# Softmax in a cross-attention and ternary feed-forward kernel: difference and scale in one VectorE step per tile, one exponential for four tiles, row sums on VectorE

## The chip, the cores and the metric

The kernel runs on 1 core of a Trainium2 chip. Its engines are TensorE (PE in the profile; PEld is its weight load), VectorE (DVE), ScalarE (ACT), GpSimd (POOL) and SyncE (SP), which issues the DMAs. The metric is the device time of one execution in microseconds; the time before is 446.84 us, the median of 3 runs (446.73 to 447.83). Less is better.

## The reference

For 8 batches of 512 rows of 512 numbers, a cross-attention over 64 context rows with a mask per batch, and then a feed-forward block with quantized activations and ternary weights:

```python
def xattn(h, mem, mask):            # h = layernorm(x), mem = ctx (8, 64, 512)
    scores = einsum('bsd,bmd->bsm', h, mem) / sqrt(512)
    scores = where(mask[:, None, :], scores, -1e30)
    attn = softmax(scores, axis=-1)
    return where(any(mask, -1)[:, None, None], einsum('bsm,bmd->bsd', attn, mem), 0)

def linear_bit(x, w, g):            # act_quant: to 8 bit by the row's largest; ternary_quant: to -1, 0, 1 times a scale
    return einsum('bsd,od->bso', act_quant(rmsnorm(x, g)), ternary_quant(w))

def ffn(h, w1, g1, w2, g2, w3, g3): # h = layernorm(x)
    return linear_bit(silu(linear_bit(h, w1, g1)) * linear_bit(h, w2, g2), w3, g3)

x = x + xattn(layernorm(x), ctx, mask)
x = x + ffn(layernorm(x), w1, g1, w2, g2, w3, g3)
```

## The kernel before

**Tiling.** Each batch is four tiles (TPB = 4) of 128 rows, 32 tiles in all. The feed-forward of a tile has four chunks (NCH = 4) of 512 hidden columns; the attention is done once for the four tiles of a batch, with tiles `sm`, `sd` and `prob` of 128 partitions x 4 tiles x 64 context rows.

**Order.** Nothing is scheduled by a planner: each engine has a program written out by hand, and semaphores tie them. Each engine runs `slot(b, j)` for tile j of batch b (`batches`, L300): slots of batch 0 from j = 2, a loop over batches 1 to 5, then batches 6 and 7 written out. In the slots of batch b the attention of batch b + 1 is made ahead, in pieces. All that lies ahead of the slots (weights brought in, scaled and clipped, attention of batches 0 and 1) is the start.

**The attention of batch a, in the order of time.** In tile 0 of batch a - 1: TensorE's `attention_ccT` and `attention_scores` (L1200), ScalarE's copy `half` (L663), TensorE's `attention_turn` (L1222); VectorE's `attention_softmax` (L881): add the mask (`sm`, L885), the largest of each row (`smax`, L888), the difference (`sd`, L892). The scores are made from x without the layernorm; the layernorm's 1/deviation comes in as the factor `rs`, one number per row and tile, which GpSimd makes in `attention` (L452 to L468) and ScalarE applies as the scale of the exponential. In tile 1: ScalarE's `attention_exp` (L665), four exponentials of 128x64, each with its own `scale` and with the row sum as an accumulated output (`psum_p`); TensorE's `attention_probT` (L1228), which transposes `prob`; ScalarE's copy `probT` (L676); VectorE's `attention_norm` (L896: reciprocal `rinv`, times `valid`: `rval`); the readout matmuls (L1243) and `attention_x1` (L904, L912), which adds the readout to X and gives the row sum of the result. The other half of the readout and of `x1` follows in tiles 2 and 3.

**The feed-forward around it.** `up` on TensorE (L1254) makes chunk n of a tile in two PSUM pairs S1 and S2; ScalarE's `silu` (L718, L724) reads S1, VectorE's gate product `gate` (L948, L954) multiplies with S2 and frees its bank (`s_hp_made`); GpSimd's `gain_3` (L526, L534) multiplies with g3 and VectorE's `max_3` (L957, L960) takes the largest. `stage_h_root`, `stage_h_factor` make the scale, ScalarE's `quantize_3` (L709, L716) quantizes the tile before, a DMA transposes it, `down` (L1281, L1297) multiplies it with W3, and VectorE's `result` (L989, L994) adds it to X. For the tile two ahead: GpSimd's `anm` (L477), which waits for that tile's x1 (`s_x1_made`), ScalarE's square (L706), GpSimd's root (L483, L488), VectorE's `ga` (`stage_a_gain`, L921, twice 128x512 with two SBUF operands), its largest (L927) and the factors (`stage_a_factor`, L939 to L945), and GpSimd's `quantize_12` (L517, L523).

**VectorE's slot** is: gate 0; `max_3` of chunk 3 of the tile before; `stage_h_top`, `stage_h_factor`; `stage_a_gain`; gate 1; (largest of `ga`, in tiles 0 to 2); gate 2; `worth_3`; `max_3` 0; `result`; gate 3; in tile 0 `attention_softmax`; `max_3` 1; `stage_a_factor`; in tile 1 `attention_norm`; in tile 2 `attention_cc`; in tile 3 the second half of x1; `max_3` 2; in tile 1 the first half of x1. **GpSimd's slot**: `gain_3` 3 of the tile before, `stage_h_root`, `anm`, `quantize_12`, `stage_a_worth`, `gain_3` 0, root, `gain_3` 1, in tile 0 `attention`, `gain_3` 2. **ScalarE's slot**: silu 0, square of the tile before, in tile 1 `attention_exp`, square for the tile two ahead, silu 1, in tile 1 the copy `probT`, in tile 0 `half` and two squares of x, then silu 2 and the two quantizations (in tiles 0 and 2 the quantizations first), silu 3, square.

The exponential and Silu lie in different activation tables, so ScalarE loads a table ahead of the exponentials and again ahead of the next Silu.

## Time and profile before

| | |
|---|---|
| median of 3 runs | 446.84 us |
| profiled execution | 446.26 us, span 444.5 us |
| mean granted TensorE clock | 0.953 |
| PE busy | 399.4 us, 90% |
| DVE busy | 404.4 us, 91% |
| ACT busy | 344.7 us, 78% |
| POOL busy | 338.4 us, 76% |
| DMA, mean rate | 149 GB/s |

The span runs from the first to the last instruction; about 2 us lie around it. A share of busy time is a mean over stages with different limits. A timeline row gives the start, the duration, the engine, the line, the operation, what it writes and reads, how many instructions are merged in the row, and in brackets the idle time before it with what ended it. Instructions of VectorE and ScalarE overlap at their ends: the next one often starts a little before the last one's duration is over.

### The profile page before, as it was taken

The page shows a single profiled execution, that of the slowest core. Times are in us where ns is not written, and L with a number is a line of the kernel's source. Part 1 is how long each engine was busy: PE and PEld are TensorE (multiplying, and loading weights), DVE is VectorE, ACT ScalarE, POOL GpSimd, SP SyncE. Part 2 cuts the span into 40 slices and gives each one's busy share as a digit, 9 for nine tenths or more (in the row PEclk, how much of TensorE's full clock was granted, in tenths as well). Part 3 has the DMA queues.
Part 4 walks back from the last instruction along what each step waited for, and adds up shares of the span by engine and source line. Part 5 has one row for each costly group of instructions (what it writes and reads, how often), then busy time and mean ns, then how long its engine had stood idle before and what let it go on. Part 6 is the DMA issues. An engine that isn't in the chain of part 4 may idle for free.

```text
span 444.5 us, 8267 instructions
## 1 busy us (share of the span) xinstructions
PE 399.4 (90%) x1870; PEld 178.8 (40%) x1870; DVE 404.4 (91%) x931; ACT 344.7 (78%) x618; POOL 338.4 (76%) x525
## 2 busy tenths in 40 slices
PE   8424695999999999999999999999999999999986
PEld 8101241334444443444344444444344434444433
DVE  5599799899999999999999999999999999999884
ACT  3678779786998689877988699868987796777651
POOL 0149888987878887878878787888788887888850
PEclk9755887999999999999999999999999999999999
DMA  6989861654774557734593477554774425354522
GB/s 263 400 300 368 296 188 24 154 94 112 188 174 100 119 117 188 179 80 106 161 204 80 111 184 179 97 118 107 191 183 76 114 57 113 83 113 98 113 66 79
DMA packets 110360, 66.41 MB, mean 149 GB/s; under 512 B 100736, under 2 KB 100864, under 8 KB 106752
## 3 DMA queue, kind: packets, MB, share of 16 engines
q1 hardware_dynamic: 110336, 66.14, 57.6%
q8 instruction: 8, 0.13, 0.1%
q14 instruction: 16, 0.13, 0.1%
HBM read 33.10 MB, written 8.39 MB: 93 GB/s over the span
## 4 chain that ended last, share of the span: by engine, by line
PE 55%; DVE 18%; issue 9%; ACT 8%; POOL 6%; DVEq 1%; DMA 1%; ACTq 0%; SPq 0%; POOLq 0%
PE S L1264 31%; PE DN L1297 16%; DVE hm L960 3%; PE R L1243 3%; DVE stageB L954 3%; ACT prob L671 2%; ACT L671 2%; POOL stageB L534 2%; PE DN L1305 2%; DVE wabs L1000 2%; DVE X L994 2%; ACT stageB L716 1%; POOL ser L563 1%; ACT junk_x L694 1%; DVE X L912 1%
## 5 line engine op out<-in xcount | busy, mean ns | idle before, releaser
L534 POOL TENSOR_TENSOR stageB<-stageB,g3b 128x512 f32<-128x512 f32 x127 | 163.1, 1292 | 32.2 <-DVE stageB L954 27.2
L1264 PE MATMUL S<-W2q,q12T 128*128 128x512 f16 x512 | 135.0, 387 | 6.0 <-DVE W2q L1029 3.6
L1264 PE MATMUL S<-W1q,q12T 128*128 128x512 f16 x512 | 134.9, 387 | 2.0 <-DVE W1q L1029 1.1
L1297 PE MATMUL DN<-W3q,stageB 128*128 128x512 f16 x496 | 122.1, 380 | 0.6 <-DVE X L994 0.3
L724 ACT ACTIVATE sg<-S,asc 128x512 f32<-128x512 f32 x128 | 87.0, 682 | 23.4 <-PE S L1264 19.7
L954 DVE TENSOR_TENSOR stageB<-sg,S 128x512 f32<-128x512 f32 x128 | 85.7, 675 | 5.9 <-ACT sg L724 4.3
L960 DVE TENSOR_REDUCE hm<-stageB 128x1 f32<-128x512 f32 x127 | 85.5, 674 | 0.1
L1264 PEld LDWEIGHTS S<-W2q,q12T 128*128 128x128 f16 x512 | 50.0, 99 | 71.5 <-DVE stageB L954 7.2
L1264 PEld LDWEIGHTS S<-W1q,q12T 128*128 128x128 f16 x512 | 48.9, 99 | 70.1 <-ACT sg L724 10.3
L731 ACT ACTIVATE junk<-stageB 128x1024 bf16<-128x1024 f32 x64 | 67.3, 1052 | 9.6 <-DVE stageB L954 9.5
L1297 PEld LDWEIGHTS DN<-W3q,stageB 128*128 128x128 f16 x496 | 48.0, 98 | 59.1 <-issue 1.6
L716 ACT ACTIVATE stageB<-stageB,hf 128x1024 f16<-128x1024 f32 x61 | 66.8, 1142 | 5.1 <-DVE hf L980 5.1
L921 DVE SCALAR_TENSOR_TENSOR ga<-X,anm,g12b 128x512 f32<-128x512 f32 x64 | 54.2, 886 | 2.4 <-POOL c L523 0.7
L523 POOL TENSOR_SCALAR c<-ga,af 128x512 f16<-128x512 f32 x64 | 45.2, 718 | 7.5 <-DVE af L945 7.4
L706 ACT ACTIVATE junk_a<-X,anm 128x512 bf16 (+1 forms) x32 | 23.0, 718 | 26.3 <-POOL anm L477 26.3
L927 DVE TENSOR_REDUCE am<-ga 128x2 f32<-128x1024 f32 x32 | 38.5, 1205 | 0.0
L488 POOL TENSOR_TENSOR ak<-avk,mhalf 128x1 f32<-128x1 f32 x32 | 27.3, 853 | 2.7
L994 DVE SCALAR_TENSOR_TENSOR X<-DN,hsc,X 128x512 f32 (+1 forms) x31 | 22.8, 737 | 2.9 <-PE DN L1297 2.9
L912 DVE SCALAR_TENSOR_TENSOR X<-R,rval,X 128x512 f32 (+1 forms) x32 | 22.6, 745 | 2.4 <-PE R L1243 2.4
L1243 PE MATMUL R<-ctxr,probT 64*128 64x512 f32 x64 | 20.9, 734 | 2.2 <-ACT probT L676 2.2
L544 POOL TENSOR_TENSOR hk<-hve,mhalf 128x1 f32<-128x1 f32 x32 | 17.6, 549 | 2.7
L483 POOL TENSOR_SCALAR avk<-avs 128x1 f32<-128x1 f32 x32 | 15.4, 481 | 3.8 <-ACT junk_a L706 1.0
(125 smaller groups left out, 425.5 us busy)
## 6 DMA issues: line engine op xcount, KB each, us to landing
X<-in_x SPq DMA_DIRECT2D x8, 1024.0 KB, 6.1
out_x<-X SPq DMA_DIRECT2D x32, 256.0 KB, 2.8
xTs<-in_xT SPq DMA_DIRECT2D x7, 1024.0 KB, 7.1
X<-in_w1T SPq DMA_DIRECT2D x4, 1024.0 KB, 10.5
stageB<-in_w2T SPq DMA_DIRECT2D x4, 1024.0 KB, 18.7
X<-in_w3T SPq DMA_DIRECT2D x4, 1024.0 KB, 9.1
ctxr<-in_ctx SPq DMA_DIRECT2D x16, 128.0 KB, 3.0
ctxc<-in_ctx SPq DMA_DIRECT2D x8, 128.0 KB, 4.4
```

Of the source, the lines that this page charges most:

```text
L523: nc.gpsimd.tensor_scalar(c12[:, i * D:(i + 1) * D], ga[:, i, :], af[:, i:i + 1], QUANTUM, ALU.mult, ALU.mult).then_inc(s_c12_made, 1)
L534: nc.gpsimd.tensor_tensor(gh[q][:, part], hp[:, part], g3b[:, part], ALU.mult).then_inc(s_gh_made, 1)
L716: nc.scalar.activation(c3[:, part], gh[q][:, part], ACT.Copy, scale=hf[:, :]).then_inc(s_c3_made, 1)
L724: nc.scalar.activation(sg[n % 2][:, :], S1[n % 2][:, :], ACT.Silu, scale=asc[z][:, 0:1])\
L731: nc.scalar.activation(junk[:, h * HALF:(h + 1) * HALF], hp[:, h * HALF:(h + 1) * HALF], ACT.Square, accum_out=hss[:, h:h + 1]).then_inc(s ...
L921: nc.vector.scalar_tensor_tensor(out=ga[:, i, :], in0=xtile(t), scalar=anm[:, :], in1=g12b[:, i, :], op0=ALU.add, op1=ALU.mult).then_inc(s ...
L927: nc.vector.tensor_reduce(am[:, :], ga[:, :, :], AX_X, ALU.max, apply_absolute_value=True)\
L954: nc.vector.tensor_tensor(hp[:, n * CH:(n + 1) * CH], sg[n % 2][:, :], S2[n % 2][:, :], ALU.mult)\
L960: nc.vector.tensor_reduce(hm[:, n:n + 1], gh[q][:, n * CH:(n + 1) * CH], AX_X, ALU.max, apply_absolute_value=True).then_inc(s_gh_max, 1)
L1243: mm = nc.tensor.matmul(R[e][:, :], probT[e * M:(e + 1) * M, i, :], ctxr[e * M:(e + 1) * M, :], start=True, stop=True)
L1264: mm = nc.tensor.matmul(bank[n % 2][:, :], q12T[q][:, i * KD + k, :], w[:, n, k, :], start=(k == 0), stop=(k == KD - 1))
L1297: mm = nc.tensor.matmul(bank[:, :], q3T[:, k, :], W3q[:, k, :], start=(k == 0), stop=(k == KH - 1))
```

## The change

Four edits that belong together:

- On VectorE `sd` is no longer one broadcast subtraction over 128x256. Four tensor_scalar instructions, one for each tile of 128x64, subtract the tile's `smax` and multiply by its `rs`. VectorE waits for `rs` (`s_rs_made`) there; ScalarE no longer does.
- On ScalarE the four exponentials of 128x64 with scale and accumulated row sum become one of 128x256 without either.
- On VectorE `attention_norm` first makes the row sums `psum_p` with a tensor_reduce over `prob`, and the reciprocal waits for it (`s_psum_made`).
- `s_prob_made` is raised once a batch, not four times, and all who wait for it (GpSimd, VectorE, TensorE) wait for the new count.

```diff
--- before.py
+++ after.py
@@ -232,6 +232,7 @@
         s_smax_made = sem("smax_made")
         s_sd_made = sem("sd_made")
         s_prob_made = sem("prob_made")
+        s_psum_made = sem("psum_made")
         s_rinv_made = sem("rinv_made")
         s_rval_made = sem("rval_made")
         s_probT_ps = sem("probT_ps")
@@ -461,7 +462,7 @@
                 nc.gpsimd.tensor_scalar(xve[:, :], var, scale, LN_EPS, ALU.mult, ALU.add).then_inc(s_x_ve, 1)
                 pool.wait_ge(s_x_ve, a + 1)
                 if later(a):
-                    pool.wait_ge(s_prob_made, TPB * a)
+                    pool.wait_ge(s_prob_made, a)
                 nc.gpsimd.tensor_tensor(xrs[:, :], xve[:, :], mhalf[:, :], ALU.pow).then_inc(s_x_rs, 1)
                 pool.wait_ge(s_x_rs, a + 1)
                 pool.nop(nofuse=True)
@@ -663,13 +664,10 @@
                 nc.scalar.copy(half[:, :], R[1][:, 0:TPB // 2 * P]).then_inc(s_half_made, 1)
 
             def attention_exp(a):
-                act.wait_ge(s_rs_made, a + 1)
                 act.wait_ge(s_sd_made, a + 1)
                 if later(a):
                     act.wait_ge(s_probT_ps, a)
-                for j in range(TPB):
-                    nc.scalar.activation(prob[:, j, :], sd[:, j, :], ACT.Exp, scale=rs[:, j:j + 1],
-                                         accum_out=psum_p[:, j:j + 1]).then_inc(s_prob_made, 1)
+                nc.scalar.activation(prob[:, :, :], sd[:, :, :], ACT.Exp).then_inc(s_prob_made, 1)
 
             def attention_probT(a):
                 act.wait_ge(s_probT_ps, a + 1)
@@ -888,14 +886,18 @@
                 nc.vector.tensor_reduce(smax[:, :], sm[:, :, :], AX_X, ALU.max).then_inc(s_smax_made, 1)
                 dve.wait_ge(s_smax_made, a + 1)
                 if later(a):
-                    dve.wait_ge(s_prob_made, TPB * a)
-                nc.vector.tensor_tensor(sd[:, :, :], sm[:, :, :],
-                                        smax[:, :].rearrange("p (j o) -> p j o", o=1).broadcast_to([P, TPB, M]),
-                                        ALU.subtract).then_inc(s_sd_made, 1)
+                    dve.wait_ge(s_prob_made, a)
+                dve.wait_ge(s_rs_made, a + 1)
+                for j in range(TPB):
+                    ins = nc.vector.tensor_scalar(sd[:, j, :], sm[:, j, :], smax[:, j:j + 1], rs[:, j:j + 1],
+                                                  ALU.subtract, ALU.mult)
+                ins.then_inc(s_sd_made, 1)
 
             def attention_norm(a):
 
-                dve.wait_ge(s_prob_made, TPB * (a + 1))
+                dve.wait_ge(s_prob_made, a + 1)
+                nc.vector.tensor_reduce(psum_p[:, :], prob[:, :, :], AX_X, ALU.add).then_inc(s_psum_made, 1)
+                dve.wait_ge(s_psum_made, a + 1)
                 nc.vector.reciprocal(rinv[:, :], psum_p[:, :]).then_inc(s_rinv_made, 1)
                 dve.wait_ge(s_rinv_made, a + 1)
                 nc.vector.tensor_scalar(rval[:, :], rinv[:, :], valid[:, bass.ds(a, 1)], None, ALU.mult)\
@@ -1226,7 +1228,7 @@
                 mm.then_inc(s_scores_ps, 1)
 
             def attention_probT(a):
-                pe.wait_ge(s_prob_made, TPB * (a + 1))
+                pe.wait_ge(s_prob_made, a + 1)
                 for i in range(TPB // 2):
                     mm = nc.tensor.transpose(R[0][:, i * P:(i + 1) * P],
                                              prob[:, 2 * i:2 * i + 2, :].rearrange("p j m -> p (j m)"), identf[:, :])
```

## Rows read from the trace of the kernel before

**Rows 1.** Busy time by stretch: length; PE, PEld, DVE, ACT, POOL; PEclk, DMA share, GB/s

```profile
128.00:176.00 48.00, 46.90 (x225) 20.71 (x224) 45.76 (x108) 40.26 (x77) 39.34 (x61) 1.00 0.60 139
```

**Rows 2.** Waits in one batch period: who, for whom: us in total, times, longest

```profile
PE R L1231 <- ACT prob L671: 1.1, 1, 1.1
...
DVE stageB L954 <- ACT sg L724: 0.6, 1, 0.6
```

**Rows 3.** The chain of waits around the exponentials: start, us, what

```profile
166.70 1.10 ACT prob L671 x6
```

**Rows 4.** Timeline of one core, from tile 3 to the next tile 0

```profile
194.88 1.27 DVE L954 TENSOR_TENSOR stageB<-sg,S 128x512 f32<-128x512 f32 x2
...
195.61 1.04 PE L1264 MATMUL S<-W2q,q12T 128*128 128x512 f16 x4
...
204.33 0.37 ACT L663 COPY half<-R 128x256 f32<-128x256 f32 x1 [0.55 <-PE R L1210]
...
208.90 0.69 DVE L954 TENSOR_TENSOR stageB<-sg,S 128x512 f32<-128x512 f32 x1 [0.61 <-ACT sg L724]
```

**Rows 5.** Timeline of tile 2; last, all instructions of L921: min/median/max ns

```profile
180.81 1.27 POOL L534 TENSOR_TENSOR stageB<-stageB,g3b 128x512 f32<-128x512 f32 x1
...
181.39 1.25 DVE L921 SCALAR_TENSOR_TENSOR ga<-X,anm,g12b 128x512 f32<-128x512 f32 x1
...
L921 DVE SCALAR_TENSOR_TENSOR ga<-X,anm,g12b x64: 737/751/1557, 21.3 to 407.1; 128x512 f32<-128x512 f32 x64
```

**Rows 6.** Timeline of the softmax of one batch, and the next batch's `sd`

```profile
162.21 2.50 POOL L534 TENSOR_TENSOR stageB<-stageB,g3b 128x512 f32<-128x512 f32 x2
...
163.71 0.42 DVE L888 TENSOR_REDUCE smax<-sm 128x4 f32<-128x256 f32 x1
...
164.26 0.73 DVE L892 TENSOR_TENSOR sd<-sm,smax 128x256 f32<-128x256 f32 x1
...
164.92 0.67 DVE L960 TENSOR_REDUCE hm<-stageB 128x1 f32<-128x512 f32 x1
...
166.35 0.35 ACT L671 ACTIVATE prob<-sd,rs 128x64 f32<-128x64 f32 x1
...
167.84 0.44 PE L1231 MATMUL R<-identf,prob 128*128 128x128 f32 x2 [1.08 <-ACT prob L671]
...
212.47 0.73 DVE L892 TENSOR_TENSOR sd<-sm,smax 128x256 f32<-128x256 f32 x1
```

**Rows 7.** Instructions of single lines: count, min/median/max ns, first and last start

```profile
L863 DVE TENSOR_SCALAR cc<-ctxc,cmean,mcol x8: 537/539/542, 6.6 to 334.7; 64x512 f32<-64x512 f32 x8
...
L1014 DVE TENSOR_SCALAR arg<-wsum x3: 133/133/134, 24.9 to 63.5; 128x1 f32<-128x1 f32 x3
...
L676 ACT COPY probT<-R x8: 350/364/373, 17.3 to 363.1; 128x256 f32<-128x256 f32 x8
...
L892 DVE TENSOR_TENSOR sd<-sm,smax x8: 424/734/837, 14.6 to 356.9; 128x256 f32<-128x256 f32 x8
...
L1022 DVE TENSOR_SCALAR W2q<-stageB,winv x1: 2341/2341/2341, 36.4 to 36.4; 128x2048 int16<-128x2048 f32 x1
L1022 DVE TENSOR_SCALAR W3q<-X,winv x1: 1278/1278/1278, 73.5 to 73.5; 128x2048 int16<-128x2048 f32 x1
```

**Rows 8.** Timeline of the row factors, the first x1 and GpSimd's next mean

```profile
176.66 0.17 DVE L899 RECIPROCAL rinv<-psum_p 128x4 f32<-128x4 f32 x1
...
178.37 0.08 DVE L912 DVE_READ_ACCUMULATOR X<-R,rval,X 128x1 f32 x1
...
178.72 0.19 POOL L477 TENSOR_SCALAR anm<-x1sum 128x1 f32<-128x1 f32 x1
```

**Rows 9.** Timeline: three waits, of the start, of batch 1 and of the tail

```profile
19.92 0.75 DVE L912 SCALAR_TENSOR_TENSOR X<-R,rval,X 128x512 f32<-128x512 f32 x1 [2.40 <-PE R L1243]
...
88.60 0.69 DVE L954 TENSOR_TENSOR stageB<-sg,S 128x512 f32<-128x512 f32 x1 [0.75 <-ACT sg L724]
...
401.64 1.04 PE L1297 MATMUL DN<-W3q,stageB 128*128 128x512 f16 x4 [0.34 <-DVE X L994]
```

## The prediction

> **What bounds the kernel now.** I read the busy shares by stretch first: in a middle stretch of 48 us TensorE is busy 46.9 us at a granted clock of 1.00 and VectorE 45.8 us [rows 1]. Neither has room to speak of, so shares cannot decide; the waits must. The waits of one batch period (48.21 us from one `sd` step to the next, from 164.26) name two: TensorE stands 1.1 us before the transposes of `prob` for the exponentials, and VectorE stands 0.6 us before one gate product for `sg` [rows 2]. The chain of waits passes through the exponentials [rows 3], which would make them worth 1 us a batch. The question is whether TensorE's time gained there reaches the end.
>
> It does not by itself. In tile 3 of each batch TensorE's second half of the last up projection starts at 195.61, and VectorE's gate product that frees its PSUM bank started at 194.88, as the first of a merged pair of 1.27 us, so it ended at about 195.55 [rows 4]. TensorE waits there for VectorE again, by some 0.1 us. From there the way is fixed: matmuls without a pause until the scores land, `half` on ScalarE at 204.33 (idle before it, waiting for the scores), two squares, the two quantizations and the third Silu, and the gate product at 208.90 after 0.61 us of waiting [rows 4]. From 194.88 to 208.90 are 14.0 us, in which nothing of the change lies. From 208.90 to the same gate product of the next batch (243.09, one period later) VectorE has no wait that the wait view shows. So the cycle that sets the period is VectorE, 34.2 us, and then this fixed 14.0 us. Whatever the change adds to VectorE between, which is both its edits, is paid; what it takes from ScalarE or TensorE there only makes TensorE wait longer at 195.61.
>
> One thing softens this: VectorE has waits that no view calls waits. When GpSimd runs its two-input product `gain_3`, a VectorE step with two SBUF operands lasts until GpSimd's is over: GpSimd's ended at 182.08, VectorE's `ga`, started 181.39, ended 182.64, 1.25 us long instead of 0.74 [rows 5]. `sd` is the same case: GpSimd's pair ended at 164.71, `sd` at 164.99, 0.28 us later, and it took 0.73 where the first batch has 0.42 [rows 6, 7]. One-input steps are held as well where they run at two columns a step: the scaling of 2048 columns took 2.34 beside GpSimd and 1.28 without [rows 7]. The Trainium skill, Advanced Engine Details and Errata, section VectorE Performance Modes, says that the second VectorE port is shared and that GpSimd and two-port instructions block each other; the trace agrees (0.28 and 0.56 us behind GpSimd's end).
>
> **The change part by part.**
>
> *One exponential.* From the first of four exponentials to TensorE's transpose: 167.84 - 166.35 = 1.49 us [rows 6]. One step of 256 columns: the copy of 256 columns takes 0.36 [rows 7], from SBUF I take 0.40 (an estimate), 0.44 with the hand-over. It saves 1.05 us of ScalarE a batch, between 0.9 and 1.1. The table load before it stays; if the compiler moves it ahead of the wait, another 1 us comes off, in the same hidden place.
>
> *`sd` as four tensor_scalar steps with two per-partition scalars.* The nearest row is `cc`, the same form over 512 columns: 0.54 [rows 7]. A step of one column without such a scalar takes 0.13 [rows 7], a reduction of 256 columns 0.42 [rows 6], some 1.1 ns a column; 512 columns at that rate would be 0.70, so `cc` runs at about two columns a step, 0.27 us, and has 0.27 fixed. A step of 64 columns is then 0.30, and since steps start 0.07 before the one ahead ends (164.92 against 164.99 [rows 6]), 0.23 from start to start; bounds 0.13 (the one-column row) and 0.30. The first is held by GpSimd to 164.71, as now, so the next instruction starts at about 164.68 + 3 x 0.23 = 165.37 instead of 164.92: +0.46 us, bounds +0.1 and +0.9 (all four held by GpSimd's small steps that follow). `sd` ends 0.46 later too. The wait for `rs` moves here from ScalarE; queued behind it are the maximum of `gh` and the factor steps of the activation scale, and GpSimd's quantization waits for these. `rs` is made early by GpSimd, ahead of the pair of [rows 6], which starts 2 us before `sd`: no cost; if it were late, all of VectorE would stand.
>
> By the Trainium skill, VectorE: DVE Perf Modes, section on the TRN2 errata, a step costs 58 cycles plus its columns over the mode's factor: 0.38 us for the four and 0.33 for the one, +0.05 instead of my +0.46, and the total would be 2.5 us less. Its rules for authors, on the other hand, ask for few instructions, which speaks against four for one. The measured 0.54 of `cc` does not fit 0.34 by that formula, so I keep the row.
>
> *Row sums.* A reduction of 128x256 like `smax`, 0.42, and the reciprocal now waits for it: 0.45 from start to start, at most the 0.55 between `smax` and `sd`, which has two waits [rows 6]. It stands ahead of `rinv` at 176.66 [rows 8]. The accumulator reads leave ScalarE (in the 1.05).
>
> *Sum on VectorE.* 0.46 + 0.45 = 0.91 us a batch. Behind it the `ga` of tile 2 at 181.39 had 0.51 us of hidden waiting for GpSimd [rows 5], which could absorb as much. But that GpSimd product comes at the end of a queue that starts with `anm` at 178.72, and `anm` needs the first `x1`, whose accumulator is read at 178.37 and 0.08 later is there [rows 8]: 178.45, now +0.91 = 179.36, so `anm` starts at about 179.45, 0.73 late, and the product with it. `ga` ends 0.73 late. So 0.73 a batch, and the other holds of `ga` follow GpSimd steps that VectorE itself releases and move along.
>
> *How often.* Batches 2 to 7: 6 x 0.73 = +4.4. Batch 1 pays 0.3 to 0.9 but has VectorE waiting 0.75 at 88.60 for a ScalarE and GpSimd queue that does not depend on it [rows 9]: 0. Batch 0 is on the way of the start: `sd` without a hold takes 0.62 more, the exponentials 1.05 less, and VectorE waits 2.40 us for the readout [rows 9], in which the reduction hides: -0.45, bounds -0.5 and 0. In the tail TensorE waits for VectorE's `X` at 401.64 [rows 9], so the delay is handed on in full.
>
> Total +4.4 - 0.45 = +3.9. The profiled execution was 446.26 us (span 444.5), the median of the runs 446.84: 450.2 or 450.7; I say 450.5.
>
> **The rivals.**
>
> *Held waits absorb it.* If GpSimd's queue in tile 2 goes by ScalarE's square instead of `anm`, VectorE gets 0.51 of its 0.91 back: 0.40 a batch, +1.95, 448.5. For it: the hold itself; against: the 178.45 against 178.72.
>
> *The 0.6 us wait goes.* If the Silu before 208.90 comes earlier because TensorE is ahead, the period grows by 0.91 - 0.69 = 0.2: +0.9, 447.4, no change. Against: the freeing gate at 195.55 fixes TensorE's lead.
>
> *TensorE is the bound (faster).* The chain of waits goes by the exponentials. If the 0.1 us at 195.61 were no true coupling and VectorE had room, each batch would win 1.05 - 0.46 = 0.59: 6 x 0.59 + 0.45 = 4.0, 442.6. It decides where the product at 194.88 ends later than TensorE is ready; only if it ends earlier is this right.
>
> *Dearer small steps.* If GpSimd's small steps hold each of the four, `sd` costs 0.9 and with the sum and fewer favours 1.1 a batch: +6.2, 452.8.
>
> That the edits don't do what they say I leave out: each replaced instruction has its row.
>
> **How the numbers follow.** Forecast 0.45, absorbed 0.14, wait gone 0.14, faster 0.13, dearer 0.14. Range 447.0 to 453.2, from the case of no change to the dear one; the faster case is left out. 0.3% (1.3 us) is about what a measurement here can tell: faster 0.13; same 0.17 (the third case and the low edge of the second); slower 0.70.
>
> **What would show it.** In the changed profile: one exponential of about 0.40; four steps of about 0.30 where `sd` was; a reduction of 0.42 before the reciprocal; TensorE's wait for `prob` gone or small and a longer one for VectorE's gate at the end of tile 3; a period of 48.9 instead of 48.21; the wait of 0.6 before the same gate product kept. The forecast is wrong if that last wait shrinks, if `ga` of tile 2 is no longer held, or if the period stays below 48.3.

## The result, and the profile after

The changed kernel takes 452.27 us, the median of 4 runs (452.02 to 452.93), against 446.79 (446.73 to 447.83, 4 runs) of the kernel before: ratio 1.0127, 95% interval 1.0114 to 1.0141, slower. The profiled execution took 452.02 us, its span 450.2 us against 444.5: +5.7 us, where the forecast's sum had +3.9. Two single executions among those of the experiments took 539.93 and 610.21 us, at granted clocks of 0.735 and 0.647; the ranges below leave them out.

Where the 5.7 us lie is read from one step that every batch has once, the maximum `smax`. Its rows of batches 1, 2 and 7 in the timeline, first of the kernel before, then of the changed one:

```profile
65.34 0.42 DVE L888 TENSOR_REDUCE smax<-sm 128x4 f32<-128x256 f32 x1
...
115.49 0.42 DVE L888 TENSOR_REDUCE smax<-sm 128x4 f32<-128x256 f32 x1
...
356.42 0.42 DVE L888 TENSOR_REDUCE smax<-sm 128x4 f32<-128x256 f32 x1
```

```profile
64.41 0.42 DVE L886 TENSOR_REDUCE smax<-sm 128x4 f32<-128x256 f32 x1
...
116.10 0.42 DVE L886 TENSOR_REDUCE smax<-sm 128x4 f32<-128x256 f32 x1
...
361.80 0.42 DVE L886 TENSOR_REDUCE smax<-sm 128x4 f32<-128x256 f32 x1
```

The difference is -0.93 at batch 1 (the start gained), +0.61 at batch 2 (batch 1 lost 1.54), +5.38 at batch 7: five periods that lost 4.77, 0.95 each (49.17 us instead of 48.22, the last one 49.01 for 48.05). The last 0.3 to 0.4 us come in batch 7 and the tail. So three terms: the period as the main one, batch 1, and the start.

**The softmax in the middle.** Timeline of the changed kernel; it answers [rows 6]:

```profile
163.78 2.50 POOL L535 TENSOR_TENSOR stageB<-stageB,g3b 128x512 f32<-128x512 f32 x2
...
165.26 0.42 DVE L886 TENSOR_REDUCE smax<-sm 128x4 f32<-128x256 f32 x1
...
165.72 1.27 DVE L892 TENSOR_SCALAR sd<-sm,smax,rs 128x64 f32<-128x64 f32 x4
...
166.91 0.67 DVE L962 TENSOR_REDUCE hm<-stageB 128x1 f32<-128x512 f32 x1
...
167.39 0.42 ACT L670 ACTIVATE prob<-sd 128x256 f32<-128x256 f32 x1
...
168.15 0.38 PE L1233 MATMUL R<-identf,prob 128*128 128x128 f32 x2
```

From `smax` to the next step `hm` VectorE takes 1.65 us, where it took 1.21 [rows 6]: +0.44 for the four steps. The one exponential takes 0.42 us, and TensorE's transposes no longer wait (no bracket behind the row; 1.08 before). The rest of the batch answers [rows 5, 8]:

```profile
178.67 0.41 DVE L899 TENSOR_REDUCE psum_p<-prob 128x4 f32<-128x256 f32 x1
...
179.11 0.18 DVE L901 RECIPROCAL rinv<-psum_p 128x4 f32<-128x4 f32 x1
...
180.84 0.08 DVE L914 DVE_READ_ACCUMULATOR X<-R,rval,X 128x1 f32 x1
...
181.19 0.19 POOL L478 TENSOR_SCALAR anm<-x1sum 128x1 f32<-128x1 f32 x1 [1.27 <-DVE X L914]
...
183.30 1.27 POOL L535 TENSOR_TENSOR stageB<-stageB,g3b 128x512 f32<-128x512 f32 x1
...
183.86 1.25 DVE L923 SCALAR_TENSOR_TENSOR ga<-X,anm,g12b 128x512 f32<-128x512 f32 x1
```

The row sums put 0.44 us ahead of the reciprocal. GpSimd's `anm` now waits 1.27 us for the first `x1`, and the product behind it still holds `ga` for 1.25 us: nothing of that hidden wait was given back.

**The waits and the fixed way.** Waits of the changed kernel over one period (175 to 224), then its timeline from tile 3 on; they answer [rows 2] and [rows 4]:

```profile
PE S L1266 <- DVE stageB L956: 1.1, 4, 0.4
DVE stageB L956 <- ACT sg L722: 0.6, 1, 0.6
PE R L1245 <- DVE X L914: 0.6, 1, 0.6
```

```profile
197.39 1.27 DVE L956 TENSOR_TENSOR stageB<-sg,S 128x512 f32<-128x512 f32 x2
...
198.12 1.04 PE L1266 MATMUL S<-W2q,q12T 128*128 128x512 f16 x4 [0.21 <-DVE stageB L956]
...
211.41 0.69 DVE L956 TENSOR_TENSOR stageB<-sg,S 128x512 f32<-128x512 f32 x1 [0.58 <-ACT sg L722]
```

TensorE's wait for the exponentials (1.1) has become 1.1 us of waits for VectorE's gate products and 0.6 for its `x1`. The way from the pair of gate products to the gate product at its end, after the scores, is 14.02 us, as before, and the wait at its end is 0.58 (0.61 before). In the profile's chain of waits VectorE has gone from 18 to 52% of the span and TensorE from 55 to 21%: the same cycle, but with TensorE now visibly behind VectorE.

**Batch 1.** The first fence is the timeline of the kernel before, the second the changed kernel's; the last line there groups the four steps of L892 between 61 and 68 us (min/median/max ns):

```profile
65.07 2.69 POOL L534 TENSOR_TENSOR stageB<-stageB,g3b 128x512 f32<-128x512 f32 x2
...
65.79 0.84 DVE L892 TENSOR_TENSOR sd<-sm,smax 128x256 f32<-128x256 f32 x1
...
66.56 0.67 DVE L960 TENSOR_REDUCE hm<-stageB 128x1 f32<-128x512 f32 x1
```

```profile
64.29 2.49 POOL L535 TENSOR_TENSOR stageB<-stageB,g3b 128x512 f32<-128x512 f32 x2
...
64.87 2.41 DVE L892 TENSOR_SCALAR sd<-sm,smax,rs 128x64 f32<-128x64 f32 x4
...
67.20 0.67 DVE L962 TENSOR_REDUCE hm<-stageB 128x1 f32<-128x512 f32 x1
...
L892 DVE TENSOR_SCALAR sd<-sm,smax,rs x4: 301/522/1300, 64.9 to 67.0; 128x64 f32<-128x64 f32 x4
```

The four steps took 2.41 us instead of 0.84. Of the four, two are 0.30 long, one 1.30, and so (the median being the mean of the middle two) one 0.74. The first product of GpSimd's pair ended at about 65.55: the 0.74 reaches from 64.87 to 65.61. The 1.30 reaches from about 65.54 to 66.84, and the second product ended at 66.78. So the narrow steps were held twice, by both products in turn.

Some 20 us later, still between `smax` 1 and `smax` 2, the same happens to two wide steps. The timeline of `ga`, in the kernel before and then in the changed one, where GpSimd's product comes between the two steps of the pair:

```profile
84.70 1.42 DVE L921 SCALAR_TENSOR_TENSOR ga<-X,anm,g12b 128x512 f32<-128x512 f32 x2 [0.65 <-POOL c L523]
```

```profile
85.13 2.43 DVE L923 SCALAR_TENSOR_TENSOR ga<-X,anm,g12b 128x512 f32<-128x512 f32 x2 [0.30 <-issue]
...
85.22 1.79 POOL L535 TENSOR_TENSOR stageB<-stageB,g3b 128x512 f32<-128x512 f32 x1
```

The pair takes 1.01 us longer, of which the shorter wait before it gives 0.35 back: 0.66 more, the second part of what batch 1 lost. Its third part is 0.16 for the row sums, of whose 0.44 the rest does not show there. VectorE's wait of 0.75 us at 88.60 [rows 9] is gone in the changed kernel and gives 0.83 back. The four steps themselves delay the next step by 1.57 (2.79 us from `smax` to `hm`, where it took 1.22). Together, 1.57 + 0.66 + 0.16 - 0.83 is 1.56, for the 1.54 us of above.

**The start.** Timeline of the kernel before, then of the changed one:

```profile
16.56 0.69 PE L1231 MATMUL R<-identf,prob 128*128 128x128 f32 x2 [2.96 <-ACT prob L671]
```

```profile
15.53 0.42 ACT L670 ACTIVATE prob<-sd 128x256 f32<-128x256 f32 x1 [0.56 <-DVE sd L892]
...
16.00 0.44 PE L1233 MATMUL R<-identf,prob 128*128 128x128 f32 x2 [2.44 <-ACT prob L670]
...
19.11 0.75 DVE L914 SCALAR_TENSOR_TENSOR X<-R,rval,X 128x512 f32<-128x512 f32 x1 [0.61 <-PE R L1245]
```

The transposes start 0.56 us earlier and are 0.25 shorter, and `x1` comes at 19.11 instead of 19.92 [rows 9]. The busy time of the stretch in which they fall (columns as in [rows 1]) shows why they are shorter; first the kernel before, then the changed one:

```profile
16.50:20.00 3.50, 2.77 (x6) 0.79 (x6) 1.07 (x4) 2.28 (x4) 0.00 (x0) 0.51 1.02 420
```

```profile
14.00:16.40 2.40, 0.40 (x2) 0.20 (x2) 2.33 (x7) 1.39 (x3) 0.00 (x0) 1.00 0.96 392
```

TensorE had been idle, and from about 16.5 us on its granted clock is 0.51, the level of 1.2 GHz, in both kernels. The transposes of the kernel before fell in the slow stretch, those of the changed kernel still ran at 2.4 GHz. That is luck and not the change: in the kept traces the clock falls anywhere from 14.6 to 17.6 us, and in the run of the changed kernel with `x1` moved (below), where it falls at 15.2, ahead of the transposes, the first `x1` comes 5.29 us after the first `smax`, not 5.06.

### The profile page after: what moved, and what is told of

It reads as the page before. It is cut to its first block, busy times and chain, and to the rows that moved or that the text cites. A ratio compares the mean times of both kernels' runs of the same rounds, so it can differ in the third digit from the quotient of the medians.

```text
span 450.2 us, 8238 instructions
## 1 busy us (share of the span) xinstructions
PE 400.4 (89%) x1870; PEld 176.7 (39%) x1870; DVE 413.5 (92%) x963; ACT 338.5 (75%) x562; POOL 337.6 (75%) x525
## 4 chain that ended last, share of the span: by engine, by line
DVE 52%; PE 21%; issue 16%; ACT 3%; DVEq 3%; POOL 2%; DMA 1%; SPq 0%; ACTq 0%; POOLq 0%
PE S L1266 11%; DVE hm L962 11%; DVE stageB L956 10%; PE DN L1299 5%; DVE ga L923 4%; DVE X L996 3%; DVE am L929 3%; DVE X L914 2%; DVE wabs L1002 2%; DVE sd L892 2%; PE DN L1307 2%; DVE aa L941 2%; DVE af L947 1%; ACT stageB L714 1%; DVE ha L976 1%
## 5 line engine op out<-in xcount | busy, mean ns | idle before, releaser
L1266 PEld LDWEIGHTS S<-W2q,q12T 128*128 128x128 f16 x512 | 48.0, 99 | 85.0 <-DVE stageB L956 25.9
L704 ACT ACTIVATE junk_a<-X,anm 128x512 bf16 (+1 forms) x32 | 23.1, 721 | 34.9 <-POOL anm L478 34.2
L478 POOL TENSOR_SCALAR anm<-x1sum 128x1 f32<-128x1 f32 x32 | 7.4, 231 | 16.7 <-DVE X L914 14.6
```

What stands on the lines that cost most here:

```text
L1266: mm = nc.tensor.matmul(bank[n % 2][:, :], q12T[q][:, i * KD + k, :], w[:, n, k, :], start=(k == 0), stop=(k == KD - 1))
```

## The experiments

Each ran beside the kernel before on the same chip (446.33 to 446.40 us there). The starts of the runs differ by up to 1.3 us from one another (the first `smax` comes at 13.22 to 14.55), so the verdict on a mechanism rests on the periods (from one `smax` to the next in the middle of the run), which agree within 0.05 us in a run, but for the first period of two kernels with a step moved (49.30 and 48.29), and the times stand beside them.

**The parts one at a time.** First the exponential alone:

```diff
+            nc.vector.memset(psum_p[:, :], 1.0)
...
-                for j in range(TPB):
-                    nc.scalar.activation(prob[:, j, :], sd[:, j, :], ACT.Exp, scale=rs[:, j:j + 1],
-                                         accum_out=psum_p[:, j:j + 1]).then_inc(s_prob_made, 1)
+                nc.scalar.activation(prob[:, :, :], sd[:, :, :], ACT.Exp).then_inc(s_prob_made, TPB)
```

> The kernel before, with one exponential of 128x256 in place of the four, and VectorE as it was. It leaves out the factor rs in the exponential and the row sums (a constant stands in for them), so that VectorE has not one instruction more. My theory (VectorE's order and the fixed way of 14.0 us behind the gate product of tile 3 set the period): the period stays at 48.2 us, TensorE's 1.1 us before the transposes of prob go and come back as waits for VectorE; only the start gains, some 1.2 us, so about 445.6 us. The rival (the chain of waits, TensorE as the bound): 1.05 us less in each of 6 batches as well, so 439 to 440 us and a period of about 47.2.

Measured: 444.39 us (444.27 to 448.8), ratio 0.9973 [0.9951, 0.9995], periods 48.22 to 48.23, unchanged. Its waits over one period:

```profile
DVE stageB L952 <- ACT sg L722: 0.6, 1, 0.6
PE S L1263 <- DVE stageB L952: 0.2, 1, 0.2
```

TensorE's 1.1 us before the transposes are down to 0.16, and nothing of it reached the period. Three waits for VectorE, 0.46 us in all (the longest is the 0.2 above), stand in its place; the rest shows as no wait. Of the 2.0 us that the profiled execution gains, 1.4 come from the start (`x1` at 18.47 instead of 19.92, 0.20 of it from the DMAs) and stand unchanged at `smax` of batch 7. The other 0.6 come behind it, where two holds of `ga` are shorter (1.28 and 1.19 us instead of 1.56 and 1.46); the theory had nothing there. That TensorE's 1.1 us are the bound is false.

Then `sd` alone: the changed kernel with four exponentials without scale, which keep the accumulated sums:

```diff
-                nc.scalar.activation(prob[:, :, :], sd[:, :, :], ACT.Exp).then_inc(s_prob_made, 1)
+                for j in range(TPB):
+                    ins = nc.scalar.activation(prob[:, j, :], sd[:, j, :], ACT.Exp, accum_out=psum_p[:, j:j + 1])
+                ins.then_inc(s_prob_made, 1)
...
-                nc.vector.tensor_reduce(psum_p[:, :], prob[:, :, :], AX_X, ALU.add).then_inc(s_psum_made, 1)
-                dve.wait_ge(s_psum_made, a + 1)
```

> The changed kernel, but with four exponentials of 128x64 that make the row sums as an accumulated output, and no reduction on VectorE: of the change only the four steps for difference and scale are left. Theory: 0.45 us more a period (48.7 us), 1 us or more in batch 1 where GpSimd's pair of products holds the first two of the four steps, and about 0.4 at the start: +3.8 us (2.8 to 4.5), so about 450.6. The rival (the price is mostly in the row sums, or in the hold of tile 2): +1.5 or less.

Measured: 449.35 us (449.0 to 450.41), ratio 1.0075 [1.0053, 1.0097], periods 48.71 to 48.73, +0.50; the +3.0 us lie in the expected range. In batch 1 its four steps took 2.23 us and pushed VectorE back by 1.39; the wait of 0.65 us before `ga` then gave 0.7 back and `ga` was not held, so `smax` 1 to `smax` 2 takes 0.65 us more than before, where the whole change costs 1.54.

And the row sums alone, on the kernel before:

```diff
-                    nc.scalar.activation(prob[:, j, :], sd[:, j, :], ACT.Exp, scale=rs[:, j:j + 1],
-                                         accum_out=psum_p[:, j:j + 1]).then_inc(s_prob_made, 1)
+                    nc.scalar.activation(prob[:, j, :], sd[:, j, :], ACT.Exp, scale=rs[:, j:j + 1]).then_inc(s_prob_made, 1)
...
+                nc.vector.tensor_reduce(psum_p[:, :], prob[:, :, :], AX_X, ALU.add).then_inc(s_psum_made, 1)
+                dve.wait_ge(s_psum_made, a + 1)
```

> The kernel before, with its four scaled exponentials, but without their accumulated sums; VectorE makes the row sums by a reduction as in the changed kernel. Theory: 0.44 us more a period (48.65 us), batch 1 nearly hidden, nothing at the start: +2.7 us (2.2 to 3.2), so about 449.5. With the start of the exponential alone, sd alone and sums alone should add up to the +5.5 of the whole change; if they do not, parts of it hide or double each other. The rival (the hold of ga in tile 2 takes the 0.44 in, as it has 0.5 us): below +0.8.

Measured: 448.01 us (447.82 to 449.23), ratio 1.005 [1.0033, 1.0067], periods 48.72 to 48.73, +0.50. Batch 1 costs it 0.17 us, nearly hidden as expected. Its +1.6 us lie below the expected range, 0.9 of that from first DMAs that landed earlier. In the period the parts add up to the whole: 0.50 + 0.50 + 0 against 0.95. In time they do not: -2.0, +3.0 and +1.6 make 2.6 of the 5.5 us. Earlier starts of the three make 1.3 of the difference. The other 1.6 are, in the traces, 0.6 before `smax` 1, 0.6 in batch 1 (only the whole change has `ga` held there) and 0.7 behind `smax` 7, less 0.3 in the periods; the first and the last of these were not followed.

**Batch 1.** To show what the narrow steps do, batch 1 alone gets back the one broadcast step. The changed kernel ran beside it once more: 451.79 us (451.04 to 452.5), ratio 1.0124 [1.0099, 1.015], periods 49.11 to 49.14.

```diff
                 dve.wait_ge(s_rs_made, a + 1)
+                if isinstance(a, int) and a == 1:
+                    nc.vector.tensor_tensor(sd[:, :, :], sm[:, :, :],
+                                            smax[:, :].rearrange("p (j o) -> p j o", o=1).broadcast_to([P, TPB, M]),
+                                            ALU.subtract).then_inc(s_sd_made, 1)
+                    return
```

> The changed kernel, but batch 1 alone makes its difference in one broadcast subtraction of 256 columns, without the factor rs (which batch 1 then lacks); batches 0 and 2 to 7 keep the four steps. Theory (the four narrow steps of batch 1 fall beside a pair of GpSimd's two-input products, and between them the second product gets in, so that two are waited for one after the other): the jump of 1.57 us at batch 1's difference falls to under 0.2, since a single step gets in between the two products as it does before; the sums and what follows keep theirs, so smax of batch 2 comes 0.5 to 1.5 us earlier than in the changed kernel (116.1), periods stay 49.17, and the time is 0.5 to 1.5 us below that of the changed kernel run beside it. Rival (batch 1's loss is the extra work and the moved half-speed stretch of the clock): the jump falls by the 0.46 of the middle batches at most, the time by at most 0.4.

Measured: 450.66 us (450.31 to 451.3), ratio to the kernel before 1.0098 [1.0077, 1.012]. Its timeline of batch 1:

```profile
64.12 2.68 POOL L535 TENSOR_TENSOR stageB<-stageB,g3b 128x512 f32<-128x512 f32 x2
...
64.70 0.97 DVE L892 TENSOR_TENSOR sd<-sm,smax 128x256 f32<-128x256 f32 x1
...
65.59 0.67 DVE L967 TENSOR_REDUCE hm<-stageB 128x1 f32<-128x512 f32 x1
```

From `sd` to `hm` 0.89 us instead of 2.33, and the jump against the kernel before is 0.14 instead of 1.57. GpSimd's pair is 0.19 us longer (2.68, as the 2.69 before, against 2.49): the single step is held by the first product and then gets in ahead of the second, for which GpSimd waits; the narrow ones end, and the second product gets in between them. 

Both traces have the same stretches at a granted clock of 0.5, about 16 to 47 and 67 to 74 us, in the run beside it 1.4 us later, and only one has the loss: the rival, the extra work and the moved stretch, is out. From the gate products ahead of `sd` to the one at 88.60, batch 1 now costs 0.17 us against the kernel before, where it costs 1.35 in the run beside it: with the hold at `sd`, that of `ga` is gone too, and the wait of 0.75 us is back. But of these 1.2 us only 0.42 are left from `smax` 1 to `smax` 2 (51.21 us against 51.63). 0.73 went in one place, two rows of the same run:

```profile
91.47 1.02 PE L1304 MATMUL DN<-W3q,stageB 128*128 128x512 f16 x4 [1.66 <-DMA stageB<-stageB]
...
112.42 0.69 DVE L961 TENSOR_TENSOR stageB<-sg,S 128x512 f32<-128x512 f32 x1 [1.34 <-ACT sg L722]
```

TensorE waited 1.66 us for the DMA that transposes the quantized tile; the transposes between 84 and 92 us took 4.8 us to land, in the run beside it 3.2, and there TensorE had no such wait. It was late from then on, and at the end of the fixed way VectorE waited 1.34 us instead of 0.61. So the hold is shown in place and size, 1.2 us; that the later transposes are what took 0.73 of it back is read from one trace. In the time the run gains 1.1 us, but its first `smax` is 0.7 us earlier, so the time does not show what the removal is worth.

The Trainium skill, SBUF — State Buffer, section Who interferes with whom, says that VectorE and GpSimd share a pair of ports by an exclusive lock. The traces agree for a lock per instruction: 0.74 and 1.30 us for two steps that take 0.30 alone.

**Can the hidden wait of `ga` be had back?** The forecast's rival said that it absorbs part of the cost. Two kernels put the first half of `x1` ahead of the maximum of chunk 2 in tile 1, so that GpSimd's `anm` comes earlier; once on the changed kernel, once on the kernel before:

```diff
-                max_3(t, 2, j % 2)
                 if attn and j == 1:
                     attention_x1(b + 1, 0)
+                max_3(t, 2, j % 2)
```

> The changed kernel, with one step moved on VectorE: in tile 1 the first half of x1 stands before the maximum of chunk 2, not behind it (0.6 us earlier); nothing is left out. Theory (GpSimd's anm waits for that x1, its product of tile 2 hangs behind anm, and that product holds VectorE's ga for 0.5 us): anm and the product 0.6 us earlier, the hold of ga in tile 2 gone, 0.5 us less in each of 6 periods than the changed kernel: 48.65 us a period, about 449.2 us in all. The rival (the hold costs nothing, or another GpSimd step holds instead): as the changed kernel, 452.2.

> The kernel before, with the same step moved on VectorE (in tile 1 the first half of x1 ahead of the maximum of chunk 2); nothing left out. In the changed kernel the move took the hold of 0.51 us away, but x1 then started 0.35 us after its turn, since it waits right behind rval. Theory: before, anm waits for GpSimd's own root as much as for x1 (the root is over at 178.59, anm starts at 178.72), so anm can come only some 0.05 us sooner, the hold stays near 0.45, and the 0.35 is paid: 48.5 us a period, +1.5 us in all, about 448. The rival (anm hangs on x1 alone): the hold goes and the period falls to 48.05, about 445.5.

Measured: on the changed kernel 450.65 us (450.39 to 450.88), ratio to the kernel before 1.0102 [1.0085, 1.0119], periods 48.97 to 49.00 (-0.17 to -0.2 against 49.17); on the kernel before 446.0 (445.48 to 446.78), ratio 0.999 [0.998, 1.0], periods 48.17 to 48.19 (-0.04). Timeline of the second:

```profile
177.46 0.75 DVE L912 SCALAR_TENSOR_TENSOR X<-R,rval,X 128x512 f32 x1 [0.25 <-DVE rval L901]
...
178.69 0.19 POOL L477 TENSOR_SCALAR anm<-x1sum 128x1 f32<-128x1 f32 x1
...
180.77 1.28 POOL L534 TENSOR_TENSOR stageB<-stageB,g3b 128x512 f32<-128x512 f32 x1
...
181.75 1.51 DVE L921 SCALAR_TENSOR_TENSOR ga<-X,anm,g12b 128x512 f32<-128x512 f32 x2
```

On the changed kernel `anm` and the product behind it come 0.3 us earlier in the period. But `x1`, directly behind `rval`, which it reads, now waits 0.24 us for it, and VectorE reaches `ga` 0.3 us later: the maximum had covered that hand-over. `ga` starts as the product ends and is not held; 0.5 of hold less 0.3 of delay is the measured gain of 0.2, where 0.5 was expected.

On the kernel before both the theory and its rival missed. The theory was right that `anm` does not hang on `x1` alone: `x1` comes 0.24 us earlier and `anm` only 0.03 (178.69 for 178.72 [rows 8]), right behind GpSimd's own root, which is over at 178.61. So the product stays where it was (180.77 for 180.81 [rows 5]). But the delay of VectorE was not paid: `ga` starts 0.36 us later than before, but the pair takes 1.51 us instead of 1.91 and is over at 183.26 for 183.30. The hold took the 0.36 in. That is the case in which the forecast's rival is right: a hold absorbs what VectorE adds behind the step that releases GpSimd (here `x1`), and nothing of what it adds ahead of it, since then GpSimd's product comes later too.

**Cheaper ways to the same end.** If VectorE's time sets the period, less work on it must shorten the kernel. First the difference made by ScalarE, as the bias of its four exponentials, with only -smax*rs (128x4) on VectorE:

```diff
-                nc.vector.tensor_tensor(sd[:, :, :], sm[:, :, :],
-                                        smax[:, :].rearrange("p (j o) -> p j o", o=1).broadcast_to([P, TPB, M]),
-                                        ALU.subtract).then_inc(s_sd_made, 1)
+                dve.wait_ge(s_rs_made, a + 1)
+                nc.vector.scalar_tensor_tensor(out=nb[:, :], in0=smax[:, :], scalar=-1.0, in1=rs[:, :],
+                                               op0=ALU.mult, op1=ALU.mult).then_inc(s_sd_made, 1)
...
+                    nc.scalar.activation(prob[:, j, :], sm[:, j, :], ACT.Exp, scale=rs[:, j:j + 1],
+                                         bias=nb[:, j:j + 1],
```

> The kernel before, with the difference taken off VectorE altogether: VectorE makes only minus smax times rs (128x4), and the four exponentials on ScalarE take it as their bias, with rs as the scale, straight from sm; sums accumulated as before. Masked scores are 65536 below, not 1e30. Theory: the 128x4 product has two SBUF operands and is held by GpSimd's pair until 164.71 like sd was, so VectorE wins only the 256 columns, 0.25 us a period: 47.95 us, and with the start about -1.5 us, 444.9. ScalarE gets 0.1 us more for each exponential and nothing depends on it. The rival (no hold for so small a step): 0.5 us a period, 443.5. If TensorE's wait for the exponentials counts: slower than before, since they take 0.4 us more.

Measured: 445.47 us (444.5 to 446.12), ratio 0.9974 [0.9963, 0.9986], periods 47.99 to 48.00, -0.22. Timeline:

```profile
161.63 2.51 POOL L534 TENSOR_TENSOR stageB<-stageB,g3b 128x512 f32<-128x512 f32 x2
...
163.59 0.57 DVE L893 SCALAR_TENSOR_TENSOR nb<-smax,rs 128x4 f32<-128x4 f32 x1
```

A step of 4 columns takes 0.57 us: it ends at 164.16, GpSimd's pair at 164.14. The hold doesn't care for the size of the step, so 256 columns less bring only 0.22.

Second the mask added by ScalarE, as a per-partition bias in its copy `half` (context rows are partitions there); VectorE's `sm` step goes, and `smax` and `sd` read the scores in PSUM:

```diff
-                nc.scalar.copy(half[:, :], R[1][:, 0:TPB // 2 * P]).then_inc(s_half_made, 1)
+                nc.scalar.activation(half[:, :], R[1][:, 0:TPB // 2 * P], ACT.Identity,
+                                     bias=mbT[:, bass.ds(a, 1)]).then_inc(s_half_made, 1)
...
-                nc.vector.tensor_tensor(sm[:, :, :], R[1][:, 0:TPB * M].rearrange("p (j m) -> p j m", j=TPB), bias,
-                                        ALU.add).then_inc(s_scores_made, 1)
-                dve.wait_ge(s_scores_made, a + 1)
-                nc.vector.tensor_reduce(smax[:, :], sm[:, :, :], AX_X, ALU.max).then_inc(s_smax_made, 1)
+                sm = R[1][:, 0:TPB * M].rearrange("p (j m) -> p j m", j=TPB)
+                nc.vector.tensor_reduce(smax[:, :], sm, AX_X, ALU.max).then_inc(s_smax_made, 1)
```

> The kernel before, with the mask added by ScalarE: the copy half becomes an Identity with a bias for each partition (there the context rows lie on the partitions), so VectorE's sm step goes, and smax and sd read the scores from PSUM. Theory: VectorE wins 0.45 us a period for sm and 0.3 for sd, which has one SBUF operand and so is not held any more: 0.75 us off VectorE in tile 0. But in tile 1 ga is held by a GpSimd product that can come only 0.26 us sooner (that long GpSimd waits for VectorE's af), so 0.3 to 0.5 us a period come through: 47.8 us, and about 443.5 us in all. The rival (holds do not matter, VectorE's busy time does): 0.75 us a period, 441.5.

> Both: the mask added in half by ScalarE, and no difference on VectorE (minus smax times rs as the bias of four exponentials that read the scores from PSUM). Masked scores are 65536 below. VectorE's softmax is one reduction and one 128x4 step. Theory: 1.0 to 1.2 us off VectorE in tile 0, but the same GpSimd product in tile 1 lets only 0.3 to 0.5 through: as the kernel with the mask in half, within 0.5 us, about 443.3. The rival (VectorE's busy time decides): 1.1 us a period, below 440.

> The changed kernel, with the mask added by ScalarE in its copy half (a bias for each of the 128 partitions) in place of VectorE's sm step; smax and the four sd steps read the scores in PSUM. Theory (VectorE's time between the gates sets the period, whatever it consists of): 0.27 off the period as the same edit gave on the kernel before, 48.9 instead of 49.17; and since smax and the four steps now start about 0.45 earlier, beside the end of GpSimd's pair, the first or first two of them are held, which could take back up to 0.5: period 48.9, range 48.8 to 49.3; time 1.5 us below the changed kernel, 0 to 2.5. Rival (reading scores in PSUM frees the four steps from the hold): period 48.5 or less, time 3 us or more below.

Measured: on the kernel before 444.67 us (444.07 to 445.45), ratio 0.9964 [0.9952, 0.9975], periods 47.95 to 47.96 (-0.27; 443.5 and 47.8 were expected), faster than both kernels. With the bias of the run above added, 446.29 (445.85 to 447.58), ratio 0.9998 [0.9986, 1.001], periods 48.12 to 48.13: worse, against what was expected. On the changed kernel 449.12 (448.81 to 449.42), ratio to the kernel before 1.0068 [1.0046, 1.009], 2.7 us below the changed kernel beside it, where 0 to 2.5 were expected, periods 48.87 to 48.88, -0.24 to -0.26. Timelines of the first, the second and the third:

```profile
162.91 2.66 POOL L533 TENSOR_TENSOR stageB<-stageB,g3b 128x512 f32<-128x512 f32 x2
...
164.68 0.42 DVE L891 TENSOR_TENSOR sd<-R,smax 128x256 f32<-128x256 f32 x1
...
169.37 2.08 DVE L920 SCALAR_TENSOR_TENSOR ga<-X,anm,g12b 128x512 f32<-128x512 f32 x2
```

```profile
164.97 0.82 DVE L893 SCALAR_TENSOR_TENSOR nb<-smax,rs 128x4 f32<-128x4 f32 x1 [0.21 <-DVE smax L888]
```

```profile
162.13 2.69 POOL L534 TENSOR_TENSOR stageB<-stageB,g3b 128x512 f32<-128x512 f32 x2
...
163.99 1.10 DVE L891 TENSOR_SCALAR sd<-R,smax,rs 128x64 f32<-128x64 f32 x4 [0.20 <-DVE smax L885]
```

With one operand in PSUM `sd` is not held: 0.42 us in the middle of GpSimd's pair, where it took 0.73 [rows 6], and the four narrow steps 1.10 instead of 1.27, beside a pair that runs to 164.82. In the second kernel the 4-column step, whose two operands lie in SBUF, is held again, for 0.82 us, and costs more than the 256 columns that it replaces. Of the 0.76 us that the edit takes from VectorE (0.45 for `sm`, 0.31 of hold) 0.27 reach the period: `ga` of tile 1 is held 0.30 longer (2.08 instead of 1.78), and VectorE's wait for `sg` grew from 0.6 to 0.8. For the third kernel the period of the theory came, but its reason, that the first steps would be held, did not. In batch 1 its steps were free too: from `smax` 1 to `smax` 2 it takes 50.32 us, in the changed kernel beside it 51.63. So moving the operand to PSUM takes 1.3 us off batch 1 (the missing `sm` step included), as the one wide step took 1.2 off up to the transposes: two different edits that both remove the hold remove the loss. The five periods bring another 1.3.

## Why the prediction was right, and where its sizes were off

**The mechanism held.** The bound was named as VectorE's 34.2 us and a fixed way of 14.0 us. The way stayed 14.02 us, its last wait 0.58, and the exponential's saving alone left the period as it was (48.22 to 48.23). Of what was to be seen, the exponential (0.42 for 0.40), the four steps (0.30 each), the reduction (0.41) and the wait kept came as said, and TensorE waits for VectorE's gates as forecast; that it now also waits 0.56 us for `x1` was not foreseen. The period is 49.17 us where 48.9 was forecast.

**`sd`, +0.46.** Right: +0.44 in the trace, +0.50 in the period alone. The row of `cc` (0.54 for 512 columns) [rows 7] carried it; the price by the Trainium skill, VectorE: DVE Perf Modes, section on the TRN2 errata, +0.05, is too low: by it a step of 64 columns takes 94 ns (an estimate from that section's formula), where the steps took 300 to 303.

**Row sums, +0.45.** Right: 0.44 in the trace, +0.50 in the period alone.

**The sum that comes through, 0.73 a batch.** Here the working failed. I took the hand-over from VectorE's `x1` to GpSimd's `anm` as nothing, and found 0.18 us of slack between 178.45 and 178.72 [rows 8]. That gap is the hand-over: after, it is 180.84 + 0.08 to 181.19, 0.27 again, with the profile's wait on it. The run with the exponential alone, where GpSimd's root is over long before, has 0.27 too. So `anm` was already waiting for `x1`, moved by the full amount, and the product and the held `ga` with it: 183.86 - 181.39 is 2.47, as `anm`'s 2.47. Nothing was absorbed: 0.95 a period, not 0.73, which is 1.1 us over five periods, and batch 7 in the tail paid 0.3 to 0.4 where I had 0.73, because two holds of `ga`, at 380 and 402 us, were 0.25 us shorter each. The run with the exponential alone has them shorter too; why was not followed. A gap that no view calls a wait can still be one.

**Batch 1, 0.** Wrong by 1.5. I had its cost at 0.3 to 0.9 and let VectorE's wait of 0.75 [rows 9] absorb it. The cost was 1.57 for `sd`, 0.16 for the sums and 0.66 for a `ga` that GpSimd's product now held. The last was in no term. The bound above for "all four held" was worked out for GpSimd's small steps. That a second 512-column product could get in between was in no term, though in the trace of before batch 1's pair ends at 67.76, 1.97 us after its `sd` begins. The wait did give back 0.83 us at the place named.

**The start, -0.45.** Too small: `x1` came 0.81 earlier, and `smax` of batch 1 0.93. I had `sd` at 0.62 more and the exponentials at 1.05 less. `sd` cost 0.45 (the exponential at 15.53 instead of 15.08), the exponential saved 1.01 (0.47 instead of 1.48 to the transposes), and 0.25 more came from the transposes running ahead of the fall of the clock, which was in no term and is luck. `smax` 1 is another 0.12 earlier: in the kept traces the way from `x1` to it takes 45.40 to 45.48 us where the granted clock is 0.5 for some 3.4 us between 55 and 61 us, as in the kernel before, and 45.26 to 45.30 where it is not, as in the changed one (but for the kernels with the mask in `half`).

The differences to my terms, 1.1 for the periods, 1.5 for batch 1, -0.5 for the start and -0.35 for batch 7, are the 1.8 us between 3.9 and 5.7. So the step that failed is the size of these terms, above all the hand-over taken as slack and the one hold assumed in batch 1; and that the sum is not further off is luck, since 2.7 us too little stand against 0.8 too much. The rival "dearer small steps" had the right place for part of the excess (narrow steps held several times), but it is batch 1 alone that does it, and there GpSimd's 512-column products, not its small steps, do the holding; in the other batches only the first step is held, by 0.30 us, since the pair is nearly over.

## What to carry to other kernels

Before moving work from one engine to another, find the cycle that sets the period, and follow it through the buffers that are freed, not only through the longest wait: the 1.1 us before TensorE were worth nothing, 0.9 us on VectorE cost 0.95. Where two engines hold each other, the number of instructions and where their operands lie count for more than their columns: keep one wide step rather than four narrow ones, and read from PSUM beside the other engine's products. A constant gap between a producer and its consumer in the timeline is a hand-over, not slack. And a hold absorbs added work only behind the step that releases the holding engine: look for that step before counting on it.

## What the runs showed of the hardware

- A VectorE step with two SBUF operands, or one of `sd`'s narrow tensor_scalar steps from SBUF to SBUF, that overlaps GpSimd's two-input product ends just behind it: 0.56 us behind for 512 columns and 0.28 for 256 [rows 5, 6], 0.06 for 64 (the 0.74 and 1.30 of batch 1), 0.02 for 4. It is held whole, whatever its size. Steps with one operand in PSUM were not held (0.42 and 0.33 to 0.34 us).
- The hold goes both ways and is decided for each instruction: behind one wide step GpSimd's second product comes 0.19 us later, between narrow steps it goes first and costs VectorE 1.0 us more. It does the same between the two wide steps of `ga` (85.13, 1.0 us more), so the boundary between steps lets it in, not their width.
- From VectorE's accumulated sum to the GpSimd step that reads it pass 0.27 us; a VectorE step directly behind the one whose 128x4 result it reads waits 0.25.
- In the start of these two profiled executions, behind an idle stretch of TensorE, the granted clock was 0.51 from about 16.5 us on, whether the first matmuls started at 16.00 or at 16.56: two transposes took 0.44 us ahead of the fall and 0.69 behind it. In the other kept traces the fall came between 14.6 and 17.6 us.
